# Where the query sums and the transposed score maxima of an attention and feed-forward block are made: folds on Pool for a DVE reduction, a DMA transpose on SP for a PE transpose and an ACT copy

## The reference

```
x = x + tanh(g_xattn) * attention(layernorm(x), ctx)
x = x + tanh(g_ffn) * ffn(layernorm(x))            # 8-bit style rounding of activations, 1024 inner

attention, per batch and head:
  Q, K, V = query @ Wq.T + bq, ctx @ Wk.T + bk, ctx @ Wv.T + bv
  qk      = Q @ K.T ; scores = qk / sqrt(16)
  feats   = [mean(scores), mean over queries of max(scores), mean over queries of var(softmax(scores))]
  log_t   = clip(MLP(feats)) ; t = exp(log_t)
  out     = softmax(qk / (2 t)) @ V ; then out @ Wo.T + bo
```

## Time and profile before

| | us |
|---|---|
| median of 3 runs (lowest, highest) | 823.28 (821.48, 824.82) |
| the profiled execution, its own time | 824.18 |
| its span, first to last instruction | 822.3 |
| granted TensorE clock over the span | 0.944 |

### The profile page before, as it was taken

The page is one execution under the profiler, slowest core; times in us unless marked ns, Lnnn a source line. Parts: engine busy times, 40 slices in busy tenths (PEclk is TensorE's granted clock), DMA queues, the critical chain, the costliest instruction groups (busy, mean ns, idle before and its releaser), DMA issues.

```text
span 822.3 us, 20941 instructions
## 1 busy us (share of the span) xinstructions
PE 714.0 (87%) x7115; PEld 478.7 (58%) x7124; DVE 721.6 (88%) x1477; ACT 692.1 (84%) x1483; POOL 521.0 (63%) x984
## 2 busy tenths in 40 slices
PE   7558899999999999999999999999998888666795
PEld 5234566666666666666666666666665556333453
DVE  5789799989989999989999999989897877679995
ACT  1578789999999999999989898999998897587693
POOL 4757566767776766676767666666751255457884
PEclk9666699999999999999999999999998999899898
DMA  9998747465757655666546675756550232345565
GB/s 200 197 253 183 172 121 149 109 119 124 147 120 149 118 148 127 128 135 131 129 122 144 121 146 120 145 125 143 115 119 8 67 93 69 77 122 135 138 159 153
DMA packets 148888, 108.50 MB, mean 132 GB/s; under 512 B 56991, under 2 KB 145183, under 8 KB 148767
## 3 DMA queue, kind: packets, MB, share of 16 engines
q1 hardware_dynamic: 143630, 101.98, 55.9%
q10 hardware_dynamic: 5152, 5.19, 2.6%
HBM read 49.54 MB, written 12.85 MB: 76 GB/s over the span
## 4 chain that ended last, share of the span: by engine, by line
PE 47%; ACT 20%; DVE 18%; issue 7%; POOL 2%; DMA 2%; SPq 1%; ACTq 0%; DVEq 0%; POOLq 0%
PE p_o L1312 9%; PE p_m L1390 9%; ACT ex L1165 7%; PE p_s L1295 7%; ACT pt L1155 6%; PE p_t L1333 5%; PE p_m L1379 4%; DVE stats L885 3%; PE p_m L1371 3%; DVE kst L1000 3%; DVE hmax L1003 3%; DVE nm L904 2%; ACT L1192 2%; PE p_m L1363 2%; ACT L1155 2%
## 5 line engine op out<-in xcount | busy, mean ns | idle before, releaser
L1165 ACT ACTIVATE ex<-p_s,nm 112x375 f32<-112x375 f32 x512 | 272.5, 605 | 10.9 <-DVE nm L904 9.8
L1155 ACT ACTIVATE pt<-p_t,ct 128x336 f32<-128x336 f32 x488 | 242.3, 563 | 33.0 <-PE p_t L1333 32.4
L885 DVE BATCH_NORM_STATS2 stats<-ex 112x6 f32<-112x375 f32 x512 | 253.0, 536 | 8.3 <-ACT ex L1165 7.0
L904 DVE TENSOR_REDUCE nm<-p_s 112x2 f32<-112x750 f32 x256 | 236.5, 924 | 2.4 <-PE p_s L1295 2.4
L1295 PE MATMUL p_s<-kst,qst 96*112 96x375 bf16 x512 | 136.0, 350 | 35.1 <-ACT ex L1165 25.3
L1333 PE MATMUL p_t<-qst,kst 99*128 99x112 bf16 x1464 | 115.4, 214 | 3.6 <-ACT pt L1155 3.0
L1333 PEld LDWEIGHTS p_t<-qst,kst 99*128 99x128 bf16 x1464 | 91.6, 98 | 42.9 <-issue 18.4
L1371 PE MATMUL p_m<-wv_sb,ctxt 128*128 128x256 f32 (+1 forms) x384 | 107.3, 403 | 4.0 <-DVE va L837 2.6
L1312 PE MATMUL p_o<-pt,va 128*32 128x112 f32 (+1 forms) x3072 | 102.6, 267 | 0.5 <-ACT ex L1165 0.5
L1390 PE MATMUL p_m<-ctxt,wk_sb 128*128 128x375 f32 x240 | 94.4, 517 | 1.1 <-DVE qf L853 0.7
L1312 PEld LDWEIGHTS p_o<-pt,va 128*32 128x32 f32 (+1 forms) x3072 | 71.0, 111 | 36.2 <-issue 30.1
(11 more groups left out here) (183 smaller groups left out, 1209.9 us busy)
## 6 DMA issues: line engine op xcount, KB each, us to landing
kst<-kp SPq DMA_DIRECT2D x378, 93.8 KB, 3.5
ctxt<-ctxt_dram SPq DMA_DIRECT2D x32, 375.0 KB, 4.2
qbounce<-qp SPq DMA_DIRECT2D x32, 168.0 KB, 2.8
qst<-qbounce SPq DMA_DIRECT2D x32, 168.0 KB, 3.6
qst<-qbounce SPq DMA_DIRECT2D x32, 112.0 KB, 3.4
xm<-x_dram SPq DMA_DIRECT2D x32, 112.0 KB, 2.4
x_dram<-x SPq DMA_DIRECT2D x32, 112.0 KB, 1.9
xt<-x_dram SPq DMA_DIRECT2D x28, 128.0 KB, 2.8
```

The lines of the kernel that those rows point to most:

```text
L885: last = nc.vector.bn_stats(stats[:, nb % RING, 2 * pb + i], ex[0:SQ, 2 * (t % 2) + i, :])
L904: nc.vector.tensor_reduce(nm[:, n % RING, 2 * p:2 * p + 2], p_s[t % 2][0:SQ, :, 0:SK], axis=AX.X, op=ALU.max, negate=True).then_inc(s_max, 1)
L1155: nc.scalar.activation(pt[:, (2 * r + i) % 8], st_home(r, i)[:, 0:KC * SQ].rearrange("k (c q) -> k c q", c=KC), ACT.Exp, scale=ct[:, nr % ...
L1165: last = nc.scalar.activation(ex[0:SQ, 2 * ((t - 1) % 2) + i, :], p_s[(t - 1) % 2][0:SQ, i, 0:SK], ACT.Exp, bias=nm[:, ne % RING, h:h + 1])
```

## The change

The query sums of batches 1 to 31 are made on Pool: one addition of the two halves of `qf` before it is overwritten, five more folds and a last addition after the split. DVE's reduction is left for batch 0 only. `nmp` is widened to 112 x 128 (the padding is set to zero once), and SP turns it with one DMA transpose in slot 1, before the context load; in slot 3 SP waits for the landing of that transpose instead of ACT's copy. The transpose and its waits leave PE, the copy leaves ACT. `st2` takes the place of `st1`, which makes room in SBUF.

```diff
--- before.py
+++ after.py
@@ -35,6 +35,8 @@
+
+FOLDS = [(SQ // 2, SQ // 2), (28, 28), (14, 14), (7, 7), (3, 4), (2, 2)]
@@ -89,12 +91,14 @@
         kf, qf = sb("kf", [P, C, SK]), sb("qf", [P, C, SQ])
+        qtree = sb("qtree", [P, C, SQ // 2])
         room = sb("kst", [P, KRING * H * SKP // 2])
@@ -103,7 +107,7 @@
         nm = sb("nm", [SQ, RING, H])
-        nmp, nmr, nmt = sb("nmp", [SQ, PARTS, H], BF16), sb("nmr", [SQ, H]), sb("nmt", [PARTS * H, SQ], BF16)
+        nmp, nmr, nmt = sb("nmp", [SQ, P // H, H], BF16), sb("nmr", [SQ, H]), sb("nmt", [P, SQ], BF16)
         ex = sb("ex", [P, 4, SK])
@@ -137,7 +141,7 @@
         wsum, wtot, wscale = sb("wsum", [P, 2, 3]), sb("wtot", [P, 3]), sb("wscale", [P, 3])
-        st2, mv2 = sb("st2", [P, TILES, 6]), sb("mv2", [P, TILES, 2])
+        st2, mv2 = st12[:, 0:TILES * 6].rearrange("p (k s) -> p k s", s=6), sb("mv2", [P, TILES, 2])
         rstd2, vpe2, sdev2 = sb("rstd2", [P, TILES]), vpe, sdev
@@ -191,7 +195,6 @@
         o_acc = p_o[:, 0:H // 4 * SQ].rearrange("p (g q) -> p g q", q=SQ)
-        t_m = p_o.ap().bitcast(BF16)[0:PARTS * H, 2 * RIDE_H:2 * RIDE_H + SQ]
         t_h1 = p_o[0:DH, RIDE_H:RIDE_H + 2 * H]
@@ -231,12 +234,13 @@
         s_qmm, s_qc, s_qs, s_qx, s_qp2 = (sem(f"s_q_{i}") for i in ("projected", "copied", "summed", "split_chain", "split"))
+        s_qt = sem("s_q_folded")
         s_vmm, s_vc = sem("s_v_projected"), sem("s_v_copied")
...
         s_s, s_max, s_e1, s_bn = sem("s_scores"), sem("s_max"), sem("s_exp1"), sem("s_bn")
-        s_mp, s_mpx, s_mt, s_mtc, s_mrow = sem("s_m_split"), sem("s_m_chain"), sem("s_m_transposed"), sem("s_m_copied"), sem("s_m_rows")
+        s_mp, s_mpx, s_mt, s_mrow, s_mpad = sem("s_m_split"), sem("s_m_chain"), sem("s_m_transposed"), sem("s_m_rows"), sem("s_m_padding")
         s_feat, s_fx, s_fr = sem("s_feats"), sem("s_feat_chain"), sem("s_feat_recip")
@@ -440,6 +444,15 @@
                 f = n + 2
+                if p == 1 and 0 <= n - 1 < B:
+
+                    b = n - 1
+                    sp.wait_ge(s_mp, count(1, b, 1))
+                    if b == 0:
+                        sp.wait_ge(s_mpad, 1)
+                    else:
+                        sp.wait_ge(s_mrow, count(16, b))
+                    sp.dma_start_transpose(nmt[:, :], nmp[:, :, :].rearrange("q r h -> q (r h)")).then_inc(s_mt, 16)
                 if p == 1 and 0 <= n and n + 3 < B:
@@ -448,8 +461,8 @@
                     b = n - 1
-                    sp.wait_ge(s_mtc, count(1, b, 1))
-                    sp.dma_start(qst[b % KRING][MROW:MROW + PARTS], nmt[:, :]).then_inc(s_mrow, 16)
+                    sp.wait_ge(s_mt, count(16, b, 16))
+                    sp.dma_start(qst[b % KRING][MROW:MROW + PARTS], nmt[0:PARTS * H, :]).then_inc(s_mrow, 16)
                 if p == 4 and 0 < f < B:
@@ -540,6 +553,7 @@
             pool.wait_ge(s_prp, PRP_LN2)
+            nc.gpsimd.memset(nmp[:, PARTS:P // H], 0.0).then_inc(s_mpad, 1)
@@ -566,13 +580,21 @@
                 nc.gpsimd.tensor_scalar(hi, qf[:, :, :], 1.0, 0.0, ALU.mult, ALU.add).then_inc(s_qx, 1)
+                summed = count(len(FOLDS), b - 1)
+                pool.wait_ge(s_qs, count(1, b))
+                nc.gpsimd.tensor_tensor(qtree[:, :, :], qf[:, :, 0:SQ // 2], qf[:, :, SQ // 2:SQ], ALU.add).then_inc(s_qt, 1)
                 pool.wait_ge(s_qx, done + 1)
-                pool.wait_ge(s_qs, count(1, b, 1))
+                pool.wait_ge(s_qt, summed + 1)
                 nc.gpsimd.tensor_tensor(qf[:, :, :], qf[:, :, :], hi, ALU.subtract).then_inc(s_qx, 1)
...
                 nc.gpsimd.tensor_tensor(lo, qf[:, :, :], mid, ALU.subtract).then_inc(s_qp2, 1)
+                for i, (width, other) in enumerate(FOLDS[1:], 1):
+                    pool.wait_ge(s_qt, summed + i)
+                    nc.gpsimd.tensor_tensor(qtree[:, :, 0:width], qtree[:, :, 0:width], qtree[:, :, other:other + width], ALU.add).then_inc(s_qt, 1)
+                pool.wait_ge(s_qt, summed + len(FOLDS))
+                nc.gpsimd.tensor_tensor(sumq[:, b % SRING, :], qtree[:, :, 0], qtree[:, :, 1], ALU.add).then_inc(s_qs, 1)
@@ -585,7 +607,7 @@
                     if b > 0:
-                        pool.wait_ge(s_mt, count(1, b))
+                        pool.wait_ge(s_mt, count(16, b))
                     nc.gpsimd.tensor_scalar(nmp[:, 0], src, 1.0, 0.0, ALU.mult, ALU.add).then_inc(s_mpx, 1)
@@ -634,6 +656,7 @@
                     nc.gpsimd.tensor_tensor(fc[:, :], ve, vo, ALU.add).then_inc(s_fx, 1)
+                    pool.wait_ge(s_qs, n)
                     nc.gpsimd.tensor_tensor(prod[:, :, :], sumq[:, t0:t0 + 2, :], sumk[:, t0:t0 + 2, :], ALU.mult).then_inc(s_fx, 1)
@@ -852,8 +875,9 @@
                                             bq[:, :].unsqueeze(2).to_broadcast([P, C, SQ]), ALU.add).then_inc(s_qc, 1)
-                    dve.wait_ge(s_qc, count(1, b, 1))
-                    nc.vector.tensor_reduce(sumq[:, b % SRING, :], qf[:, :, :], axis=AX.X, op=ALU.add).then_inc(s_qs, 1)
+                    if b == 0:
+                        dve.wait_ge(s_qc, count(1, b, 1))
+                        nc.vector.tensor_reduce(sumq[:, b % SRING, :], qf[:, :, :], axis=AX.X, op=ALU.add).then_inc(s_qs, 1)
                 if p == 4 and 0 <= m5 < B:
@@ -1128,12 +1152,6 @@
                     nc.scalar.activation(ct[:, r0:r0 + 2].rearrange("p b h -> p (b h)"), ltc[:, :], ACT.Exp, scale=-1.0, bias=ln2[:, 0:1]).then_inc(s_c, 1)
-                if p == 2 and 0 <= n - 1 < B:
-                    b = n - 1
-                    act.wait_ge(s_mt, count(1, b, 1))
-                    if b > 0:
-                        act.wait_ge(s_mrow, count(16, b))
-                    nc.scalar.copy(nmt[:, :], t_m).then_inc(s_mtc, 1)
                 if p == 4 and 0 <= m < B:
@@ -1338,17 +1356,8 @@
                     pe.wait_ge(s_lt, (n - 1) // 2)
-                if p == 3 and 0 <= n - 1 < B:
-                    pe.wait_ge(s_mtc, count(1, n - 1, 1))
                 if weighted and p != 7:
                     pv()
-                if p == 1 and 0 <= n - 1 < B:
-                    if n == 1:
-                        pe.wait_ge(s_pre, IDB)
-                    if 0 <= n - O_LAG - 1:
-                        pe.wait_ge(s_oc, min(n - O_LAG, B))
-                    pe.wait_ge(s_mp, count(1, n - 1, 1))
-                    nc.tensor.transpose(t_m, nmp[:, :, :].rearrange("q r h -> q (r h)"), identb[0:SQ, 0:SQ]).then_inc(s_mt, 1)
                 if p == 7 and pair_of(n):
@@ -1434,6 +1442,7 @@
                     if i == 0:
+                        pe.wait_ge(s_pre, IDB)
                         pe.wait_ge(s_e1, SLOTS * B)
```

More of the change, by code:

```diff
@@ L90, in gated_block @@
         hmask = sb("hmask_sb", [P, HG])
-        st1, mv = sb("st1", [SQ, B, 6]), sb("mv", [SQ, B, 2])
+        st12, mv = sb("st12", [P, B * 6]), sb("mv", [SQ, B, 2])
+        st1 = st12[0:SQ, :].rearrange("p (b s) -> p b s", s=6)
         rstd, vpe, sdev = sb("rstd", [SQ, B]), sb("vpe", [P, B]), sb("sdev", [P, B])
```

## The result

The changed kernel takes 826.55 us (median of 20 runs, 822.52 to 831.59) against 823.04 us (820.82 to 825.11) for the kernel before, measured beside it: ratio 1.0045, 95% interval [1.003, 1.006]. It is slower by some 3.7 us where the prediction had it faster by 2.1. The profiled execution took 824.8 us, its span is 822.9.

The account below looks back on a forecast made before the run. No single engine bounds it: PE, ACT and DVE are each 93 to 94% busy. 824.18 - 4.2 - 0.2 - 1.2 + 2.2 + 1.3 = 822.1, less 0.9 gives 821.2 us; range for 8 in 10: 814 to 828.

Parts of the forecast that it names:

- The end of the start's term: At the start, Pool's folds delay batch 1's K-stack DMAs, for which PE stands still: +2.2 us taken, ends 0 and +2.2.
- Memset, padding, the new place of `st2`: Pool does these once or behind work it has itself just ended: cost nothing.
- PE's transpose, -4.2: Removing PE's transpose from the two full PE stretches gains 26 steps x 0.16 us: -4.2, ends 0 and -4.2.
- the second rival: The transpose's 0.16 us are not gained, since PE then waits for ACT: 825.4 us, chance 0.13.
- -4.2 - 0.2 + 1.3 = -3.1: Terms for PE's transpose removed (-4.2), ACT's copy removed, in the drain (-0.2), and SP's wait in the first rows (+1.3).
- DVE's query sum, -1.2: DVE's reductions of batches 1 to 31 removed; only three lie on the chain of waits, 0.41 us each: -1.2.
- The first rival: DVE paces after all, so each removed reduction counts: some 814 us, chance 0.12.
- Pool's folds in the rows, 0: In the rows, some 2.2 us of folds per batch fit into Pool's idle time: cost 0.
- The +0.9 at 72.95: At 72.95 us Pool has only 1.27 us idle, so the folds push `xn` and PE by +0.9.
- SP's +1.3: In the first rows SP waits for the DMA transpose's landing, making a load late for DVE: +1.3 us.
- the slow one at 828: SP is held by the transpose's landing in the first rows, delaying loads and the next K stack: 828 us, chance 0.18.
- The forecast's own range: Around 821.2 us, from 818.8 (the start costs nothing) to 823.5; the forecast had chance 0.52.

Follow-up runs that it names:

- transpose_only_aligned: Changed kernel without Pool's folds (DVE sums every batch), DMA transpose kept, K and query stacks at multiples of 256 bytes as in the kernel before; ratio 0.997.
- no_sums: Changed kernel with the transpose back on PE and no query sums after batch 0 on DVE or Pool, key sums read instead; ratio 1.0015.
- layout_only: Kernel before with only tile sizes changed (wider maxima tile, shared statistics tile), no zeroing of padding, no DMA transpose; ratio 1.0012.
- padding_only: Kernel before with the wider maxima tile, the shared statistics tile and Pool's one zeroing of the padding, no DMA transpose; ratio 1.0018.
- folds_only: Kernel before with Pool's folds in place of DVE's query sums for batches 1 to 31, transpose on PE and copy on ACT kept; ratio 1.0089.

## Why the prediction failed, step by step

- **The end of the start's term.** The prediction had the folds' cost for batch 1 between 0 and +2.2, the latter "it moves with the issue", and reasoned that "what joins a queue later leaves it later". The 2.2 us of issue were right (I rose by 2.2 to 2.3 us, with the address held or not). The landing grew as well, and PE lost 4.1 us with the address held (25.83 to 29.95). In time it is 1.0029 against 0.997 on one chip, 4.8 us, good to some 2.5. This is the step that failed: the earlier trace rows show a landing of 10.9 us, and I didn't ask what filled the queue, nor whether it would be delayed too. ACT's weight loads were not: they even left 1.07 us earlier, counted from the eviction, since DVE's sum was gone, a side of the change that the prediction didn't see. Beside them the late stack lost more than its delay; with one of the loads moved it did not (2.4 us of issue, 1.9 at PE). The upper end should have been open, and the mend was visible: nothing needs a query sum that early. Putting the folds behind the keys gives 0.69% back with the address held (1.0029 to 0.996), 5.7 us, good to some 2.5. W shows 2.6 of it and the wait for `xn` 0.9; the rest is not located.
- **"Memset, padding, the new place of `st2`: nothing."** As work they are nothing. As addresses they were not priced at all: the folds' tile moves every tile behind it by 448 bytes. The price is 1.0045 against 1.0029 for the changed kernel, 0.9999 against 0.997 and 0.9982 against 0.996 for the other two, 1.3 to 2.4 us, each good to some 2.3.
- **PE's transpose, -4.2.** Mis-sized. The gain is 0.15 us in an even row and nothing in an odd one, where PE waits for ACT: the second rival, true for half of the rows. From batch 10 to batch 31 the changed kernel gains 1.07 us (405.03 to 403.96) in 21 rows. The whole move to the transposing transfer is worth 0.3%, some 2.5 us, where its terms said -4.2 - 0.2 + 1.3 = -3.1. In the profile of `transpose_only_aligned` 1.2 us of it lie between the evictions of batches 10 and 31, and 1.1 between those of batches 1 and 10, which one execution can't hold.
- **DVE's query sum, -1.2.** Not seen: `no_sums` (1.0015) is no faster than `layout_only` (1.0012). Each is known to 0.2%, so 1.2 us, 0.15%, can't be excluded by the times. The first rival, DVE as the pace-maker at 814, is excluded.
- **Pool's folds in the rows, 0.** Right. By form (count | busy us, mean ns | idle) the seven additions take 424, 304, 237, 220, 201, 203 and 195 ns, 1.8 us, of which three rows:

```profile
L585 POOL TENSOR_TENSOR qtree<-qf 128x112 f32<-128x112 f32 x31 | 13.1, 424 | 0.0
L595 POOL TENSOR_TENSOR qtree<-qtree 128x56 f32<-128x56 f32 x31 | 9.4, 304 | 0.0
...
L595 POOL TENSOR_TENSOR qtree<-qtree 128x6 f32<-128x6 f32 x31 | 6.2, 201 | 2.4
```

 With the hand-overs it is the idle time of the earlier trace rows, and the pair didn't lengthen. The +0.9 at 72.95 was right as a wait: PE's for `xn` grew by 0.9 us, though no run prices it alone. The sum left it out, as running beside SP's +1.3, which was not seen.
- **SP's wait.** +1.3 for the first rows was not seen: adding the transposes to `padding_only` changed nothing that can be told (1.0018 both, each known to 0.2%). Two rivals came near the measured 826.55 by luck: the second at 825.4, whose mechanism is true for half of the rows but whose sum lacks the loss in the start, and the slow one at 828, by SP's hold, which no run shows as a cost.
- **The forecast's own range.** 821.2 without the start's 2.2 us is 819.0, not 818.8, and for 823.5 no working is given.

Summed anew, from the runs (each term good to some 2.5 us): transfer -2.5, folds +4.8 and address +1.3 make +3.6; measured +3.7. This is no check of the account, as the three terms are the steps between the same runs. The forecast of 821.2 missed the sign; the time is within the range of 814 to 828.

## What to carry to other kernels

Work that fits into an engine's idle time in the steady state can still stand ahead of the first transfer that everything waits for: read the start by itself, and put optional work behind it. Where a landing is several times the usual, list who else has transfers in flight and whether they move with the change. And when a change adds a tile, look at where the tiles behind it come to lie: declare it last, or compare the DMA engines' busy share for the same packets.

And an engine that is relieved of work reaches what stands behind it earlier, its transfers' issues too: ask what those then collide with.

Both lessons together, the folds behind the keys and the tile behind the stacks, give `folds_behind_k_aligned`, 0.996 [0.9939, 0.9981], which does all that the change does and is faster than both kernels. Whether later weights add to it was not tried.

## What I had not expected of the hardware

- Packets of the same number and size took 55.9% or 66.7% of the engines' span, by where the stacks and the tiles behind them lay: on a multiple of 256 bytes or 224 bytes above one (65.2 and 66.3% in `folds_only` and `no_sums`, 192 above). The steady rows hardly felt it (38.65 against 38.68 us a pair); the first ones, when PE stood waiting for a stack, did.
- A delay of 2.2 to 2.3 us in a transfer's issue became 4.1 to 5.5 us at PE, while loads of 1 MB on another engine's queue were in flight, one of which now left 1.07 us earlier. With another of these loads issued 7 us later, the time to landing fell from 14.05 to 9.7 us, and 2.4 us of issue cost PE 1.9.
